# Token scatters of a cross-attention stage, issued one at a time behind exponentials and values products

## The chip, the cores and the metric

The kernel runs on one core of a Trainium2 chip. Its engines are TensorE (PE in the profile, PEld for its weight loads), VectorE (DVE), ScalarE (ACT), GpSimd (POOL) and SyncE (SP, whose queue issues the plain DMAs). The metric is the device time of one launch in microseconds (us); lower is better.

## The reference, cut to what matters

Input x is 32 batches of 256 tokens with 256 features. Three sublayers follow each other, each with a residual sum and a layer norm: self attention with 16 heads and rotary embedding; a differential cross attention (two softmaxes per head over 120 context keys, subtracted with a factor lambda); and a mixture of experts that routes each token to the best 6 of 64 experts.

```
x = layernorm(x + attention(x))
x = layernorm(x + differential_cross_attention(x, ctx))   # 16 heads, 2 softmaxes each, 120 keys
scores = sigmoid(x @ router.T); top_idx = top_k(scores + bias, 6)
x = layernorm(x + sum_of_6_experts(x, top_idx) + shared_mlp(x))
```

To gather the tokens of an expert later, the kernel fills a table in HBM during the cross stage: entry (expert, position) holds a token's number. Each batch has 256 tokens x 6 choices; on chip that is 2 groups of 128 tokens, so 2 x 6 = 12 scatters per batch, each of which writes 128 four-byte entries, one per partition.

## The kernel before, in words

The program has a self stage, a cross stage and an expert stage. In the first two, every engine runs its own instruction list, and semaphores order them. The cross stage works on one batch of 256 tokens per step, and a step holds work of several batches at different depth (a software pipeline): `A` is the batch whose queries and keys are projected and split into three bf16 parts, `B` and `M` those whose row maxima are found, `S` the one with scores, exponentials and values products, `O` the one with output projection and residual, `R` the one with norm, transposition and router, and `Q` the one whose slots are sorted and scattered. The lags against the step number are A 1, B 2, M 3, S 4, O 5, R 6, Q 7, for 32 batches. So Q and S are both on in steps 7 to 35, which are 29 steps. The last three steps with scatters have no S.

A step has eight rounds g = 0 to 7, on TensorE in this order: scores of round g (two heads, both softmaxes; L810, `c_sc`), a set of maximum scores (L828, `c_mx`), and the values product of the round before (L846, `c_pv`), with the projections, transpositions and router products of the other batches in between. ACT turns the scores of a round into exponentials (L1172, `c_exp`), copies two rounds of values to `att_o_raw` (L1182, `c_pvc`), and takes the rest in a written order: in round 3 the first bf16 part (`copy_parts0`, L1205, `c_hi`), in round 5 `oT` (L1306), the second part (`copy_parts1`, L1209, `c_mid`), and the copy of the transposed negative maxima (`att_cross_nmaxT`, L1318, behind TensorE's L1020 by `c_mTp`), and after that the exponentials of round 6. DVE reduces each set of maximum scores (L1434, `c_red`, which TensorE needs before the next set) and normalises the transposed rounds (L1445, L1447, L1456, behind L861 by `c_ot`).

GpSimd has in each step: two small operations on token numbers, the twelve scatters of Q (L1704, from `scatter`), the first subtraction of A (L1751, waits for `c_hi`; its result is wanted by L1209), the second subtraction (L1759, waits for `c_mid`; its end `c_lo` lets SP store the parts), the norm's small operations for O (L1769 to L1776, behind DVE's statistics) and two sums for R (L1783). Its list is run strictly in the order in which it is written. A scatter is an indirect DMA for which GpSimd itself writes the descriptors. `scatter_in_round(Q, S, g, at)` first waits until the exponentials of round g of the batch S are done, and then issues all scatters of `at`.

Of the kernel before, what the change touches and what calls it, by code (L numbers as in the profile page):

```python
# [101 lines left out]
def attention(nc, n_batches, x_in, xT_in, W, ctxT_in, CW, consts, y_out, res_out, z_out, yT_out, table, moe):  # L102
# [24 lines left out]
    for is_q in (True, False):  # L127
        part_of = [pair[0 if is_q else 1] for pair in PAIRS]
        at = 0
# [20 lines left out]
    NGR = 8  # L150
# [9 lines left out]
    C_N_INIT = 9  # L160

    C_STACK_LOADS = []
    for is_q in (True, False):
        part_of = [pair[0 if is_q else 1] for pair in PAIRS]
        at = 0
# [15 lines left out]
    with ExitStack() as ctx:  # L181
# [1453 lines left out]
        def _(pool):  # L1635
# [73 lines left out]

            def scatter_in_round(Q, S, g, at):  # L1710
                if S.on:
                    n_exp = held(pool, NGR * S.n + g + 1)
                    pool.wait_ge(c_init, C_N_INIT)
                    pool.wait_ge(c_exp, n_exp)
                scatter(Q, at)

            def cross_step(at_lag):
# [9 lines left out]
                if Q.on:  # L1727
                    pool.tensor_scalar(tok_f[:, :], tok_f[:, :], float(T), None, ALU.add).then_inc(c_tk, 1)
                    n_tk, n_scat = held(pool, Q.n + 2), held(pool, 16 * TC * TOP * Q.turn)
                    n_now = held(pool, Q.n + 1)  # L1730
                    pool.wait_ge(c_init, C_N_INIT)
                    pool.wait_ge(c_tk, n_tk)
                    if past(Q.n, 3):
                        pool.wait_ge(c_scat[Q.slot], n_scat)
                    pool.tensor_copy(tok_i[:, Q.slot, :], tok_f[:, :]).then_inc(c_tok, 1)
                    if S.on:
                        n_exp = held(pool, NGR * S.n + 1)
                    pool.wait_ge(c_init, C_N_INIT)
                    pool.wait_ge(c_tok, n_now)
                    pool.wait_ge(c_slot, n_now)  # L1740
                    if S.on:
                        pool.wait_ge(c_exp, n_exp)
                    scatter(Q, range(0, 1))
                    scatter_in_round(Q, S, 1, range(1, 3))
                yield
# [6 lines left out]
                if Q.on:  # L1752
                    scatter_in_round(Q, S, 2, range(3, 4))
                    scatter_in_round(Q, S, 3, range(4, 6))
                    scatter_in_round(Q, S, 4, range(6, 7))
                yield
# [3 lines left out]
                if Q.on:  # L1760
                    scatter_in_round(Q, S, 5, range(7, 9))
                    scatter_in_round(Q, S, 6, range(9, 10))
                if O.on:
# [20 lines left out]
                if Q.on:  # L1784
                    scatter_in_round(Q, S, 7, range(10, 12))

# [426 lines left out]
```

## Time and profile before

| | us |
|---|---|
| median of 3 runs (lowest, highest) | 2097.91 (2096.47, 2111.97) |
| the profiled execution | 2095.74 |
| its span, first to last instruction | 2093.9 |
| its time outside of the span | 1.84 |

The page splits the span into 40 slices of 52.3 us. The self stage fills about the first 14 of them, the cross stage those from there to about slice 32, and the expert stage the rest. A row of the timeline gives the start, the duration, the engine, the line and what is written and read; in brackets stands how long the engine was idle before it and what released it. "remote" is a releaser that the profile could not name, "issue" is time in which it shows no wait. Matmul ends are modelled by the profiler.

### The profile page before, as it was taken

To read this page: it belongs to the slowest core of one execution; us is meant where nothing else is said; L and a number is where in the kernel's file an instruction comes from. 1 tells how busy PE (TensorE), PEld (TensorE's weight loads), DVE (VectorE), ACT (ScalarE), POOL (GpSimd) and SP (SyncE) were. 2 spreads that over 40 slices of the span, in tenths; PEclk is the share of its full clock that TensorE was granted. 3 is DMA by queue.
4 is the path that set the end of the run, shared out by engine and by line. 5 is a ranking of instruction groups with operands and counts; after the bars stand their busy time and mean duration, and the time that the engine had idled before them with its cause. 6 is when DMAs were issued, how large, how long until landed. Compare 5 with 4: busy or idle time off the path is not lost. (4 is left out here: it accounts for less than half of the span.)

```text
span 2093.9 us, 45046 instructions
## 1 busy us (share of the span) xinstructions
PE 1740.5 (83%) x14560; PEld 1217.1 (58%) x14560; DVE 1273.1 (61%) x2887; ACT 1083.7 (52%) x1701; POOL 1274.3 (61%) x1303
## 2 busy tenths in 40 slices
PE   4799999999999877888888888887888833999985
PEld 2566666666766644555555555555554422888874
DVE  3566676767677755776767766677766530322265
ACT  1466666666666555665555565565655410111134
POOL 4566776767677421466566565666665564677676
PEclk7899999999999998998888888899887656999998
DMA  5677868778787655555555445555445104787687
GB/s 121 152 178 185 186 175 187 180 190 188 178 194 177 164 119 125 121 107 108 117 111 103 91 100 115 110 106 115 102 91 99 37 25 123 178 201 195 146 286 266
DMA packets 322362, 300.94 MB, mean 144 GB/s; under 512 B 80626, under 2 KB 299572, under 8 KB 313040
## 3 DMA queue, kind: packets, MB, share of 16 engines
q1 hardware_dynamic: 299728, 286.56, 57.4%
q0 software_dynamic: 22528, 13.03, 4.0%
q8 instruction: 59, 0.97, 0.2%
q14 instruction: 47, 0.39, 0.1%
HBM read 187.28 MB, written 111.17 MB: 143 GB/s over the span
## 5 line engine op out<-in xcount | busy, mean ns | idle before, releaser
L1704 POOL DMA_INDIRECT slot_table<-att_cross_tok_i,att_cross_slot_i x384 | 382.2, 995 | 145.0 <-issue 95.8
L1344 DVE TENSOR_REDUCE att_nmax<-self_p_mx 128x2 f32<-128x512 f32 x512 | 329.3, 687 | 205.6 <-PE self_p_mx L628 205.1
L1434 DVE TENSOR_REDUCE att_cross_nmax<-self_p_mx 128x8 f32<-128x960 f32 x256 | 295.5, 1154 | 178.3 <-PE self_p_mx L828 109.8
L1079 ACT ACTIVATE att_probs<-self_p_sc 128x1024 f32<-128x1024 f32 x256 | 261.0, 1020 | 98.8 <-PE self_p_sc L616 96.3
L1172 ACT ACTIVATE att_probs<-self_p_sc 120x1024 f32<-120x1024 f32 x256 | 261.8, 1023 | 43.0 <-PE self_p_sc L810 31.1
L628 PE MATMUL self_p_mx<-att_k_stack,att_q_stack 96*128 96x256 bf16 x1024 | 161.0, 277 | 55.3 <-DMA att_k_stack<-self_k_parts 50.3
L846 PE MATMUL self_p_pv<-att_probs,att_v_aug 120*32 120x256 f32 x2048 | 187.3, 442 | 5.3 <-ACT att_o_raw L1182 4.9
L828 PE MATMUL self_p_mx<-att_k_stack,att_q_stack 48*128 48x120 bf16 x2048 | 112.5, 231 | 83.5 <-DVE att_cross_nmax L1434 52.8
L616 PE MATMUL self_p_sc<-att_q_stack,att_k_stack 99*128 99x256 bf16 x1024 | 158.3, 278 | 11.6 <-ACT att_probs L1079 10.0
L1980 PE MATMUL ffn_ph<-ffn_xT,ffn_sw 128*128 128x256 f32 x512 | 119.2, 387 | 47.9 <-DMA ffn_x_sb<-x_and_gates 47.9
L828 PEld LDWEIGHTS self_p_mx<-att_k_stack,att_q_stack 48*128 48x128 bf16 x2048 | 77.7, 104 | 127.6 <-DVE att_cross_nmax L1434 77.4
L628 PEld LDWEIGHTS self_p_mx<-att_k_stack,att_q_stack 96*128 96x128 bf16 x1024 | 96.1, 98 | 83.8 <-DMA att_k_stack<-self_k_parts 34.8
L1751 POOL TENSOR_TENSOR att_qk_rest<-att_qk,att_parts 128x752 f32<-128x752 f32 x32 | 51.9, 1622 | 151.3 <-ACT att_parts L1205 150.1
L643 PE MATMUL self_p_pv<-att_probs,att_v_aug 128*32 128x256 f32 x2048 | 141.9, 396 | 0.6 <-ACT att_probs L1079 0.6
L616 PEld LDWEIGHTS self_p_sc<-att_q_stack,att_k_stack 99*128 99x128 bf16 x1024 | 87.0, 98 | 91.2 <-ACT att_probs L1079 42.6
L1663 POOL TENSOR_TENSOR att_rope_products<-att_qkb,att_cos_t 128x512 f32<-128x512 f32 x32 | 40.9, 1277 | 154.5 <-ACT att_qkb L1095 154.5
L1971 PE MATMUL ffn_p<-ffn_sw,ffn_hT 128*128 128x256 f32 x512 | 119.3, 387 | 18.6 <-ACT ffn_hT L2010 17.9
L1980 PEld LDWEIGHTS ffn_ph<-ffn_xT,ffn_sw 128*128 128x128 f32 x512 | 97.9, 194 | 61.2 <-issue 48.1
L1182 ACT ACTIVATE att_o_raw<-self_p_pv 128x512 f32<-128x512 f32 x128 | 76.8, 600 | 107.4 <-PE self_p_pv L846 89.0
L810 PE MATMUL self_p_sc<-att_q_stack,att_k_stack 51*128 51x256 bf16 x1024 | 111.6, 301 | 16.6 <-ACT att_probs L1172 16.0
L2095 POOL DMA_INDIRECT expert_sums<-ffn_ye,ffn_slots x64 | 92.2, 1440 | 44.5 <-DMA expert_sums<-ffn_ye,ffn_slots 18.1
L1971 PEld LDWEIGHTS ffn_p<-ffn_sw,ffn_hT 128*128 128x128 f32 x512 | 95.8, 192 | 36.2 <-ACT ffn_hT L2010 23.1
(174 smaller groups left out, 3632.3 us busy)
## 6 DMA issues: line engine op xcount, KB each, us to landing
att_q_stack<-self_q_parts SPq DMA_DIRECT2D x64, 256.0 KB, 5.6
expert_sums<-att_zeros SPq DMA_DIRECT2D x64, 256.0 KB
att_q_stack<-cross_q_parts SPq DMA_DIRECT2D x128, 128.0 KB
ffn_w<-in_ffn_w SPq DMA_DIRECT2D x64, 256.0 KB
ffn_m_sb<-expert_sums SPq DMA_DIRECT2D x32, 512.0 KB, 5.4
self_q_parts<-att_parts SPq DMA_DIRECT2D x32, 384.0 KB, 2.8
self_k_parts<-att_parts SPq DMA_DIRECT2D x32, 384.0 KB, 3.8
att_k_stack<-self_k_parts SPq DMA_DIRECT2D x32, 384.0 KB, 8.0
```

The source lines that it names most:

```text
L616: mm = pe.matmul(p_sc[:, w, kc * T:(kc + 1) * T], k_stack[0:RM, S.slot, k_at:k_at + P], q_stack[0:RM, S.slot, u * T:(u + 1) * T], start=Tr ...
L628: mm = pe.matmul(p_mx[:, m % 2, c * T:(c + 1) * T], q_stack[0:RK, M.slot, q_at:q_at + P], k_stack[0:RK, M.slot, m * T:(m + 1) * T], start= ...
L643: mm = pe.matmul(p_pv[j * SLOT:(j + 1) * SLOT, (p % 2) * T:(p % 2 + 1) * T], v_aug[:, S.slot, kc, u, :], probs[:, (u // 2) % 4, (2 * (u % ...
L828: mm = pe.matmul(p_mx[:, e, (2 * hh + c) * KEYS:(2 * hh + c + 1) * KEYS], q_stack[r:r + C_RK, M.slot, q_at:q_at + P], k_stack[r:r + C_RK, ...
L846: mm = pe.matmul(p_pv[j * SLOT:(j + 1) * SLOT, (g % 2) * T:(g % 2 + 1) * T], v_aug[0:KEYS, S.slot, e, 2 * g + hh, :], probs[0:KEYS, g % 4, ...
L1079: act.activation(probs[:, g % 4, :], p_sc[:, :, :].rearrange("p b n -> p (b n)"), ACT.Exp, scale=SCALE).then_inc(s_exp, 1)
L1172: act.activation(probs[0:KEYS, g % 4, :], p_sc[0:KEYS, :, :].rearrange("p b n -> p (b n)"), ACT.Exp, scale=C_SCALE).then_inc(c_exp, 1)
L1344: dve.tensor_reduce(nmax[:, M.slot, :, m], p_mx[:, m % 2, :].rearrange("p (c k) -> p c k", c=TC), AX_X, ALU.max, negate=True).then_inc(s_r ...
L1434: dve.tensor_reduce(cnmax[:, M.slot, :, :, 2 * m:2 * m + 2].rearrange("p c e h -> p e h c"), p_mx[:, :, 0:4 * KEYS].rearrange("p e (x k) - ...
L1704: pool.indirect_dma_start(out=table[:, :], out_offset=bass.IndirectOffsetOnAxis(ap=slot_i[:, Q.slot, tc, k:k + 1], axis=0), in_=tok_i[:, Q ...
L1971: mm = pe.matmul(p_y[:, tc * DM:(tc + 1) * DM], hT[:, b % 2, k, tc * P:(tc + 1) * P], sw2[:, k, :], start=(k == 0), stop=(k == SK - 1))
L1980: mm = pe.matmul(p_h[:, k // 2, (k % 2) * T:(k % 2 + 1) * T], sw1[:, f, k * P:(k + 1) * P], xT[:, t % 3, f, :], start=(f == 0), stop=(f == ...
```

## The change

The helper that issued a group of scatters behind the exponentials of a round is replaced by two: one waits for the exponentials of round g, the other for the values product of round g (`c_pv`), and each issues one scatter. By position in GpSimd's list:

| place in GpSimd's list | before | after |
|---|---|---|
| ahead of the first subtraction (L1751) | 0 (exp 0); 1, 2 (exp 1) | 0 (exp 0); 1 (exp 1); 2 (values 1); 3 (exp 2); 4 (values 2); 5 (exp 3) |
| ahead of the second subtraction (L1759) | 3 (exp 2); 4, 5 (exp 3); 6 (exp 4) | 6 (exp 4); 7 (values 4) |
| ahead of the norm's operations | 7, 8 (exp 5); 9 (exp 6) | 8 (exp 6); 9 (values 6) |
| at the end | 10, 11 (exp 7) | 10 (exp 7); 11 (values 7) |

```
-            def scatter_in_round(Q, S, g, at):
+            def scatter_behind_exp(Q, S, g, at):
                 if S.on:
                     n_exp = held(pool, NGR * S.n + g + 1)
                     pool.wait_ge(c_init, C_N_INIT)
                     pool.wait_ge(c_exp, n_exp)
-                scatter(Q, at)
+                scatter(Q, range(at, at + 1))
+
+            def scatter_behind_values(Q, S, g, at):
+                if S.on:
+                    n_pv = held(pool, NGR * S.n + g + 1)
+                    pool.wait_ge(c_init, C_N_INIT)
+                    pool.wait_ge(c_pv, n_pv)
+                scatter(Q, range(at, at + 1))
...
-                    scatter_in_round(Q, S, 1, range(1, 3))
+                    scatter_behind_exp(Q, S, 1, 1)
+                    scatter_behind_values(Q, S, 1, 2)
+                    scatter_behind_exp(Q, S, 2, 3)
+                    scatter_behind_values(Q, S, 2, 4)
+                    scatter_behind_exp(Q, S, 3, 5)
...
-                    scatter_in_round(Q, S, 2, range(3, 4))
-                    scatter_in_round(Q, S, 3, range(4, 6))
-                    scatter_in_round(Q, S, 4, range(6, 7))
+                    scatter_behind_exp(Q, S, 4, 6)
+                    scatter_behind_values(Q, S, 4, 7)
...
-                    scatter_in_round(Q, S, 5, range(7, 9))
-                    scatter_in_round(Q, S, 6, range(9, 10))
+                    scatter_behind_exp(Q, S, 6, 8)
+                    scatter_behind_values(Q, S, 6, 9)
...
-                    scatter_in_round(Q, S, 7, range(10, 12))
+                    scatter_behind_exp(Q, S, 7, 10)
+                    scatter_behind_values(Q, S, 7, 11)
```

## Rows read from the trace of the kernel before

**Rows 1.** The page: busy shares, and the scatters' group

```profile
PE 1740.5 (83%) x14560; PEld 1217.1 (58%) x14560; DVE 1273.1 (61%) x2887; ACT 1083.7 (52%) x1701; POOL 1274.3 (61%) x1303
...
L1704 POOL DMA_INDIRECT slot_table<-att_cross_tok_i,att_cross_slot_i x384 | 382.2, 995 | 145.0 <-issue 95.8
```

**Rows 2.** Busy times of two steps, each from one second subtraction to the next

```profile
1224.30:1253.40 29.10, 24.36 (x240) 15.39 (x237) 19.87 (x49) 16.81 (x28) 17.67 (x23) 0.88 0.49 104
1395.70:1422.80 27.10, 22.27 (x233) 14.04 (x233) 19.76 (x50) 16.64 (x28) 17.56 (x23) 0.94 0.60 112
```

**Rows 3.** Waits from 1000 to 1400 us: total, times, longest

```profile
ACT att_o_raw L1182 <- PE self_p_pv L846: 42.5, 18, 3.3
...
ACT att_cross_nmaxT L1318 <- remote: 31.1, 13, 3.0
...
DVE att_cross_o_inv L1445 <- remote: 28.2, 27, 2.4
```

**Rows 4.** Timeline of a cross step before the first scatter

```profile
831.04 0.42 PE L1020 MATMUL self_p_k<-att_identb,att_cross_nmax_parts 128*96 128x128 bf16 x2
...
831.50 0.38 ACT L1318 ACTIVATE att_cross_nmaxT<-self_p_k 96x256 bf16<-96x256 bf16 x1 [7.14 <-PE self_p_k L1020]
```

**Rows 5.** Timeline of GpSimd in the step that starts at about 1230 us

```profile
1239.74 1.04 POOL L1704 DMA_INDIRECT slot_table<-att_cross_tok_i,att_cross_slot_i  x1 [0.87 <-POOL att_cross_tok_i L1735]
...
1242.37 0.98 POOL L1704 DMA_INDIRECT slot_table<-att_cross_tok_i,att_cross_slot_i  x1 [0.30 <-issue]
1246.74 1.62 POOL L1751 TENSOR_TENSOR att_qk_rest<-att_qk,att_parts 128x752 f32<-128x752 f32 x1 [3.39 <-ACT att_parts L1205]
1248.51 1.03 POOL L1704 DMA_INDIRECT slot_table<-att_cross_tok_i,att_cross_slot_i  x1 [0.15 <-issue]
...
1252.40 0.98 POOL L1704 DMA_INDIRECT slot_table<-att_cross_tok_i,att_cross_slot_i  x1 [0.30 <-issue]
1253.39 1.64 POOL L1759 TENSOR_TENSOR att_parts<-att_qk_rest,att_parts 128x752 bf16<-128x752 f32 x1
...
1257.79 0.98 POOL L1704 DMA_INDIRECT slot_table<-att_cross_tok_i,att_cross_slot_i  x1 [0.30 <-issue]
1262.18 0.21 POOL L1769 TENSOR_SCALAR att_cross_var_eps<-att_cross_mv 128x2 f32<-128x2 f32 x1 [3.41 <-issue]
```

**Rows 6.** Timeline of the other engines in the same step

```profile
1242.62 0.60 ACT L1182 ACTIVATE att_o_raw<-self_p_pv 128x512 f32<-128x512 f32 x1 [1.18 <-remote]
...
1247.75 0.66 DVE L1582 CAST att_cross_nmax_parts<-att_cross_nmax 128x64 bf16<-128x64 f32 x1
...
1249.61 0.65 PE L861 MATMUL self_p_tok<-att_ident,att_o_raw 128*128 128x128 f32 x4
...
1250.10 0.28 PE L1020 MATMUL self_p_k<-att_identb,att_cross_nmax_parts 128*96 128x128 bf16 x2
...
1250.57 0.84 ACT L1209 ACTIVATE att_parts<-att_qk_rest 128x752 bf16<-128x752 f32 x1
1250.71 1.16 DVE L1434 TENSOR_REDUCE att_cross_nmax<-self_p_mx 128x8 f32<-128x960 f32 x1
...
1252.82 1.99 PE L1035 MATMUL self_p_q<-att_cross_w_o,att_oT 128*128 128x256 f32 x8
...
1254.30 0.26 DVE L1445 RECIPROCAL att_cross_o_inv<-self_p_tok 128x16 f32<-128x16 f32 x1 [2.42 <-remote]
1254.42 0.38 ACT L1318 ACTIVATE att_cross_nmaxT<-self_p_k 96x256 bf16<-96x256 bf16 x1 [3.01 <-remote]
...
1254.70 1.01 ACT L1172 ACTIVATE att_probs<-self_p_sc 120x1024 f32<-120x1024 f32 x1
...
1255.77 0.39 PE L810 MATMUL self_p_sc<-att_q_stack,att_k_stack 51*128 51x256 bf16 x4 [0.96 <-ACT att_probs L1172]
...
1258.17 0.64 PE L846 MATMUL self_p_pv<-att_probs,att_v_aug 120*32 120x256 f32 x8
...
1260.24 0.60 ACT L1182 ACTIVATE att_o_raw<-self_p_pv 128x512 f32<-128x512 f32 x1 [3.02 <-PE self_p_pv L846]
```

## The prediction, made before the changed kernel ran

> **What bounds the kernel now.** I read the page first. No engine is full: TensorE 83%, GpSimd 61%, VectorE 61%, ScalarE 52% [rows 1]; the edit touches only the cross stage, so I went on to that. The table of busy times by stretch gives the period of one step: 29.10 us, or in some stretches 27.10 us, with TensorE busy for 24.4 and 22.3 us of it and GpSimd for 17.6 [rows 2]. The stage is therefore bound by a chain of handoffs between engines, and the question is which of them are late. The waits by pair over 400 us answer it: ACT stands idle 42.5 us for values products, 31.1 us for the transposed maxima, and DVE 28.2 us for transposed rounds, all three released by TensorE [rows 3]. Per step (about 14 in that stretch) that is 3.0, 2.2 and 2.0 us, though they overlap one another.
>
> The reader should now compare two handoffs of the same kind. Before the first scatter of the program, the transposition L1020 ends at 831.04 + 0.42 = 831.46 and ACT copies at 831.50: 0.04 us [rows 4]. In a step with scatters the same transposition ends at 1250.10 + 0.28 = 1250.38, ACT is free at 1250.57 + 0.84 = 1251.41, and yet it starts at 1254.42: 4.04 us after the producer, 3.01 of them idle. DVE's L1445 is the same: its input ends at 1250.26 and it starts at 1254.30 [rows 6]. Between the two lies a run of four scatters back to back, from 1248.51 to 1253.38; both consumers start 0.9 to 1.0 us after it is over [rows 5, 6]. The same is seen twice more in that step. The copy L1182 starts at 1242.62, while the third scatter of a run is being issued (from 1242.37), and at the step's end the values product ends at 1258.81, a scatter at 1258.77, and ACT starts at 1260.24, 1.43 us late [rows 5, 6]. So the trace reads as if TensorE's completion signals do not get through while a scatter's transfers follow its issue, for about 1 us each; in a run the shadows join up, and the several signals that TensorE gives in rounds 5 and 6 queue behind them. Signals from ACT or DVE to TensorE are prompt: scores L810 start at 1255.77, 0.06 us behind the exponentials of 1254.70, in the shadow or the issue of a scatter [rows 6]. This is an inference from times; the cause is not in the rows.
>
> The Trainium skill, page "SBUF — State Buffer", section "Who interferes with whom", says the opposite: a DMA never contends with a compute engine, and only a VectorE operation that takes the shared port starves descriptor writing. By that rule scatters could stand anywhere and the change would be worth nothing (2098 us). The rule covers data ports, not the passing of signals; the 0.04 against 4.04 us speaks for an effect, so I keep it as a rival.
>
> **The change, part by part.** Nothing is added or removed but semaphore waits: the twelve scatters stay, 384 in all at 995 ns [rows 1]. The waits on exponentials before were mostly void, because GpSimd came to them late. It was held in its list by `c_hi`: scatter 3 was allowed behind the exponentials of round 2, but stood behind the first subtraction, which began at 1246.74 after 3.39 us of idleness. Thus 3 to 6 ran as one block of four [rows 5]. After the change:
>
> *Ahead of the first subtraction.* Scatters 0 and 1 as before. Scatter 2 waits for the values product of round 1, whose signal reached ACT at 1242.62; so it starts at about 1242.7 instead of 1242.37. Scatter 3 follows, to about 1245.0 (two issues of 0.98 with 0.30 between). Scatter 4 waits for values 2, TensorE's own signal, in the shadow of 3: about 1 us after that, 1245.6 to 1246.0. Scatter 5 follows, to about 1248. The first subtraction then starts at 1248.0 instead of 1246.74, 1.3 us late, and takes 1.62 to 1249.6. The user of its result, L1209, starts at 1250.57 because ACT is busy before it, so 0.9 us of cover are left and it costs nothing [rows 5, 6]. DVE's cast at 1247.75 took 0.66 us, ending just after the subtraction; a later subtraction can hold up the four small operations there, and with them the reduction at 1250.71, by up to 1 us; and ACT's copies in rounds 2 and 3 get three more shadows in their neighbourhood. Bounds for both: 0 (TensorE has several us of dense work in these rounds and its consumers have slack) and 1.0 us. I take 0.3, nearer to zero, since a single shadow is shorter than a round of about 2.5 us.
>
> *Between the subtractions.* Two scatters (6, 7) instead of four, with 7 behind TensorE's signal of values 4, so a run cannot build up. The transposed maxima would then pass at once or after one shadow: ACT's idle time of 3.01 us (2.4 on average, 31.1 / 13) falls to at most 1.0 [rows 3, 6]. Not all of that arrives: the next scores L810 stand in TensorE's list behind the projection L1035, which ends at 1252.82 + 1.99 = 1254.81, and they start at 1255.77. So 0.96 us is what this gives before TensorE itself is late next [rows 6]. The reduction L1434 at 1250.71 and the matmuls behind it come no earlier, and if they came earlier too, the bound of this term would be the whole 1.4 to 2.0 us.
>
> *Behind the second subtraction.* It may start at about 1251.5 instead of 1253.39, since GpSimd has nothing else left; SP takes its result in order behind the maxima's rows, so this alone gains nothing. Scatter 8 moves from exponentials 5 to 6 and 9 from exponentials 6 to values 6, ending about 1 us earlier or later than before: GpSimd waited 3.41 us for the norm's statistics at 1262.18, which covers it [rows 5]. The 1.43 us at the step's end stay, because scatter 9 still ends about when values 7 do. Zero. Scatters 10 and 11 stay late behind the norm; zero.
>
> *TensorE's clock.* The step of 29.10 us has a mean granted clock of 0.88 and the one of 27.10 has 0.94 [rows 2]; of the two levels, 1.2 and 2.4 GHz, each step spends part of its time in the lower one. Fewer gaps on TensorE should make more steps like the faster one: between 0 and 2.0 us per step. I take 0.6, nearer to zero, because no row says which gap lowers the clock, and the one at the step's end (1260.24) stays.
>
> Sum per step: 0.96 - 0.3 + 0.6 = 1.3 us, rounded down to 1.2 for the waits that a scatter now has on signals that themselves come late. It counts in the 29 steps with both S and Q: 35 us. Against the profiled execution that is 2095.7 - 35 = 2061; the median of the runs is 2.2 above that execution, so 2063.
>
> **The rivals.** *It gives nothing* (the first rival, also what the named rule says). The shadow sits on whatever signal comes next; twelve scatters cost about the same wherever they lie, so what rounds 5 and 6 win, rounds 2 and 3, now with scatters 3, 4 and 5, lose. For it: ACT waited in rounds 1 to 2 as well (1.18 us at 1242.62). Against it: in the middle of the step the engines have work queued and GpSimd stood idle there. 2098, plus or minus 10.
>
> *It becomes slower: the first subtraction is late.* All of 2 to 5 now stand ahead of it, and two of them wait for TensorE's signals, which are the ones that shadows hold up. Its end was 1246.74 + 1.62 = 1248.36 and ACT's turn for L1209 is at 1250.57, a slack of 2.21 us. If scatters 4 and 5 are each one shadow later than I think, the subtraction ends at about 1251.6 and ACT, which runs its list in order, stands at L1209 with the maxima's copy and the exponentials of round 6 behind it. That is 1.0 us per step over the slack, 29 us: 2127. It decides from a subtraction that ends later than 1250.6. For it: it takes only 0.9 us more than my estimate. Against it: the gain of the second part stays and would pay for most of it, so about 2110 is as likely within this case.
>
> *It becomes much faster:* the gain of the second part arrives in full and most steps reach the 27.10 us of the faster ones: (0.96 + 2.0) x 29 = 86 us, 2012.
>
> **How the numbers follow.** My forecast with its own range 2020 to 2085 has 0.48, the much faster case 0.10, nothing 0.25, slower 0.17. What a measurement of this kernel can tell from no change is about 1%, 21 us: faster means under 2077. Most of the first two cases lie there (0.55), slower than 2119 has 0.14, and 0.31 is left. The range takes in the bounds of the unshown costs, 2018 to 2112; what it leaves out is the end of either extreme case.
>
> **What would show it.** In the profile after: GpSimd's scatters in runs of one or two (three at most); the wait of L1318 with the releaser not named down from 2.4 us per step to under 1.0; the first subtraction starting one to two us later against its `c_hi`, with no wait of L1209 for it; the period near 27.5 to 28; the copies L1182 and L1266 in rounds 2 and 3 with waits up to 1 us. The prediction is wrong if L1318 still waits 2 us in spite of short runs (then the shadow is no such thing), if ACT waits for L1751 (second rival), or if new waits of ACT in rounds 2 to 4 add up to what rounds 5 and 6 win (first rival).

## The result, and the profile after

| | before | after |
|---|---|---|
| median of 18 runs each (us) | 2098.84 | 2117.67 |
| span of the profiled execution | 2093.9 | 2116.3 |
| mean granted clock | 0.901 | 0.901 |

The ratio is 1.0091, with a 95% interval of 1.0073 to 1.0109: slower by 19 us, where 35 us less were forecast. The page after, the busy line and the scatters' group, to be read beside [rows 1]:

```profile
PE 1750.2 (83%) x14560; PEld 1219.9 (58%) x14560; DVE 1305.2 (62%) x2887; ACT 1083.6 (51%) x1701; POOL 1274.3 (60%) x1303
...
L1704 POOL DMA_INDIRECT slot_table<-att_cross_tok_i,att_cross_slot_i x384 | 381.8, 994 | 301.4 <-PE self_p_pv L846 157.5
```

The same instructions ran, 2887 on VectorE, and yet VectorE was busy for 32 us more. That is the line to follow. The waits from 1000 to 1400 us, against [rows 3]:

```profile
POOL slot_table L1704 <- PE self_p_pv L846: 79.7, 30, 5.7
ACT att_probs L1172 <- PE self_p_sc L810: 43.1, 26, 3.6
ACT att_o_raw L1182 <- PE self_p_pv L846: 39.3, 28, 2.5
...
DVE att_cross_nmax L1434 <- remote: 26.5, 12, 2.8
ACT att_cross_gate_e L1278 <- remote: 21.6, 8, 5.3
```

L1318's wait with the releaser not named is gone, as forecast, but L1434 and L1278 have such waits instead. Over 866 to 1600 us these unnamed waits of ACT and DVE sum to 126.4 us before and 125.9 after: they moved and did not shrink.

To see where in a step time was lost, take the starts of the eight exponentials (L1172) in the timeline and average their distances over the 25 steps whose batch `S` is 5 to 29, for the period and for four stretches of a step (us). Below stands how much of each stretch TensorE spent at the lower of its two clock levels, worked out from the mean granted clock (1 less it, times 2, times the length):

| | period | rounds 0 to 3 | 3 to 5 | 5 to 7 | 7 to 0 |
|---|---|---|---|---|---|
| before | 28.50 | 12.41 | 4.83 | 7.09 | 4.18 |
| after | 29.35 | 11.04 | 6.42 | 8.86 | 3.03 |
| at the lower clock, before | 7.4 | 6.5 | 0.3 | 0.5 | 0.0 |
| at the lower clock, after | 7.5 | 2.1 | 1.2 | 4.1 | 0.1 |

2.5 us are won and 3.4 lost; 0.85 us x 29 steps is 25 us, about the difference of the spans (22). The mean clock is the same, but the time at the lower level has moved from rounds 0 to 3 into round 6. Now VectorE by form of instruction, 866 to 1266 us (busy, mean ns of one), first before, then after:

```profile
L1456 DVE TENSOR_TENSOR att_rope_products<-att_cross_o_n 128x128 f32<-128x128 f32 x56 | 27.1, 484 | 1.9
...
L1582 DVE CAST att_cross_nmax_parts<-att_cross_nmax 128x64 bf16<-128x64 f32 x14 | 5.6, 402 | 0.5
```

```profile
L1456 DVE TENSOR_TENSOR att_rope_products<-att_cross_o_n 128x128 f32<-128x128 f32 x54 | 24.0, 444 | 1.9
...
L1582 DVE CAST att_cross_nmax_parts<-att_cross_nmax 128x64 bf16<-128x64 f32 x14 | 12.9, 922 | 0.5
...
L1584 DVE TENSOR_TENSOR att_cross_nmax_rest<-att_cross_nmax,att_cross_nmax_parts 128x64 f32<-128x64 f32 x14 | 11.6, 830 | 0.5
...
L1466 DVE TENSOR_TENSOR att_cross_gate_b<-att_cross_gate,att_cross_e_bias 128x128 f32<-128x128 f32 x14 | 5.5, 390 | 0.5
```

A single L1582 usually takes 0.20 us, L1584 0.22, L1456 and L1466 0.29. The timeline of one step after shows what happens to them:

```profile
1188.05 1.04 POOL L1704 DMA_INDIRECT slot_table<-att_cross_tok_i,att_cross_slot_i  x1 [0.86 <-ACT att_probs L1172]
...
1191.61 1.16 DVE L1434 TENSOR_REDUCE att_cross_nmax<-self_p_mx 128x8 f32<-128x960 f32 x1 [1.90 <-remote]
...
1191.99 0.98 POOL L1704 DMA_INDIRECT slot_table<-att_cross_tok_i,att_cross_slot_i  x1 [0.30 <-issue]
...
1194.02 0.28 ACT L1278 ACTIVATE att_cross_gate_e<-self_p_q 128x128 f32<-128x128 f32 x1 [2.35 <-remote]
...
1196.25 2.34 DVE L1584 TENSOR_TENSOR att_cross_nmax_rest<-att_cross_nmax,att_cross_nmax_parts 128x64 f32<-128x64 f32 x1
...
1196.86 1.64 POOL L1762 TENSOR_TENSOR att_qk_rest<-att_qk,att_parts 128x752 f32<-128x752 f32 x1
...
1198.53 0.83 ACT L1209 ACTIVATE att_parts<-att_qk_rest 128x752 bf16<-128x752 f32 x1 [0.53 <-POOL att_qk_rest L1762]
...
1199.57 0.38 ACT L1318 ACTIVATE att_cross_nmaxT<-self_p_k 96x256 bf16<-96x256 bf16 x1 [0.22 <-PE self_p_k L1020]
...
1200.99 1.62 POOL L1769 TENSOR_TENSOR att_parts<-att_qk_rest,att_parts 128x752 bf16<-128x752 f32 x1
...
1201.65 0.58 PE L828 MATMUL self_p_mx<-att_k_stack,att_q_stack 48*128 48x120 bf16 x8 [1.87 <-DVE att_cross_nmax L1434]
...
1203.17 3.78 PE L1035 MATMUL self_p_q<-att_cross_w_o,att_oT 128*128 128x256 f32 x8
...
1207.53 1.02 ACT L1172 ACTIVATE att_probs<-self_p_sc 120x1024 f32<-120x1024 f32 x1 [3.55 <-PE self_p_sc L810]
```

L1584 takes 2.34 us instead of 0.22 and ends 0.09 us after GpSimd's first subtraction (L1762 in the changed file) does. Its successors on the way to the transposed maxima, and the next reduction, are late by as much, and TensorE stands idle for 1.87 us ahead of L828 until that reduction is done. Then it runs slowly: the granted clock over L1035 is 0.50 here, and L1035 takes 3.78 us, where it took 1.99 at a granted clock of 1.00 in [rows 6]. Both go into the wait of 3.55 us ahead of the exponentials of round 7. L1035 ran mostly at the lower level in 18 of the 25 steps after and in 3 before; its mean went from 2.21 to 3.13 us.

Summed over the timelines of the same 25 steps (duration over the usual one, losses of 0.25 us and more, where a GpSimd subtraction lies beside), the *stretch* of VectorE's operations is 0.64 us a step before and 2.05 after. The first subtraction used to start 0.11 us after its input was ready (`c_hi`) and now starts 3.8 us after, because three more scatters stand ahead of it and some of them wait for values products (GpSimd waits 79.7 us for these in 400; in e1 below, without such waits, the subtraction starts 2.3 us after). There it meets L1584 or L1582 in 19 of 25 steps.

The rows from 1188.05 to 1194.02 show the other loss. The run of four scatters, 3 to 6, between the subtractions is gone, but scatters 0 to 3 now go out back to back in 21 of 25 steps, since their signals have already come when GpSimd gets to them. L1434 and L1278 have their unnamed waits during this run and just behind it: such waits of ACT and DVE were mostly in round 5 before (3.7 us a step) and are mostly in round 3 after (4.3), and there rounds 3 to 5 lose 1.6 us.

### The profile page after: what moved, and what is told of

The parts are those of the page before. It is cut to its first block and busy times, and to the rows that moved or that the text cites. A ratio compares the mean times of both kernels' runs of the same rounds, so it can differ in the third digit from the quotient of the medians.

```text
span 2116.3 us, 45246 instructions
## 1 busy us (share of the span) xinstructions
PE 1750.2 (83%) x14560; PEld 1219.9 (58%) x14560; DVE 1305.2 (62%) x2887; ACT 1083.6 (51%) x1701; POOL 1274.3 (60%) x1303
## 5 line engine op out<-in xcount | busy, mean ns | idle before, releaser
L1434 DVE TENSOR_REDUCE att_cross_nmax<-self_p_mx 128x8 f32<-128x960 f32 x256 | 295.2, 1153 | 170.8 <-PE self_p_mx L828 75.5
L1172 ACT ACTIVATE att_probs<-self_p_sc 120x1024 f32<-120x1024 f32 x256 | 262.2, 1024 | 109.5 <-PE self_p_sc L810 102.6
L828 PE MATMUL self_p_mx<-att_k_stack,att_q_stack 48*128 48x120 bf16 x2048 | 108.5, 231 | 85.0 <-DVE att_cross_nmax L1434 48.9
L828 PEld LDWEIGHTS self_p_mx<-att_k_stack,att_q_stack 48*128 48x128 bf16 x2048 | 75.5, 103 | 123.8 <-DVE att_cross_nmax L1434 72.2
L1182 ACT ACTIVATE att_o_raw<-self_p_pv 128x512 f32<-128x512 f32 x128 | 76.8, 600 | 96.9 <-PE self_p_pv L846 84.1
L810 PE MATMUL self_p_sc<-att_q_stack,att_k_stack 51*128 51x256 bf16 x1024 | 109.5, 296 | 13.8 <-ACT att_probs L1172 13.3
L1762 POOL TENSOR_TENSOR att_qk_rest<-att_qk,att_parts 128x752 f32<-128x752 f32 x32 | 52.2, 1631 | 78.5 <-ACT att_parts L1205 78.0
```

The source lines that it names most:

```text
L828: mm = pe.matmul(p_mx[:, e, (2 * hh + c) * KEYS:(2 * hh + c + 1) * KEYS], q_stack[r:r + C_RK, M.slot, q_at:q_at + P], k_stack[r:r + C_RK, ...
L1172: act.activation(probs[0:KEYS, g % 4, :], p_sc[0:KEYS, :, :].rearrange("p b n -> p (b n)"), ACT.Exp, scale=C_SCALE).then_inc(c_exp, 1)
L1434: dve.tensor_reduce(cnmax[:, M.slot, :, :, 2 * m:2 * m + 2].rearrange("p c e h -> p e h c"), p_mx[:, :, 0:4 * KEYS].rearrange("p e (x k) - ...
```

## The experiments

Beside each of them the kernel before ran on the same chip. Theories 1, 2 and 3 of the expectations are explained in those of e1 and e4, theories C (collision) and L (lateness) in that of e13. They were made on five chips; on two of them, those of e5 to e8 and of e9 to e12, the kernel before takes 1954 us instead of 2100. Ratios are to the kernel before on that chip. "Period" and "stretch" are per step, as above.

| run | before, us | this, us | ratio, 95% | period | stretch |
|---|---|---|---|---|---|
| e1_place | 2101.5 | 2141.2 | 1.021 (1.016 to 1.026) | 30.10 | 1.55 |
| e2_waits | 2101.5 | 2098.2 | 0.999 (0.996 to 1.002) | 28.62 | 0.63 |
| e3_memset | 2101.5 | 2052.1 | one run | 27.83 | 1.34 |
| e4_memset_after | 2101.5 | 2034.0 | one run | 27.17 | 2.41 |
| e5_none | 1954.3 | 1961.2 | one run | 25.51 | 1.10 |
| e6_nosub_before | 1954.3 | 1991.3 | 1.019 (1.015 to 1.022) | 25.30 | 1.24 |
| e7_nosub_after | 1954.3 | 2000.3 | 1.025 (1.022 to 1.027) | 25.43 | 1.49 |
| e8_after_345_memset | 1954.3 | 2006.2 | one run | 25.86 | 2.05 |
| e9_before_again | 1953.4 | 1955.2 | 1.000 (0.996 to 1.003) | 24.02 | 0.32 |
| e10_after_again | 1953.4 | 2071.5 | 1.061 (1.057 to 1.065) | 28.44 | 3.40 |
| e11_five | 1953.4 | 2022.1 | 1.037 (1.032 to 1.042) | 26.42 | 2.11 |
| e12_three | 1953.4 | 2003.5 | 1.026 (1.022 to 1.030) | 26.16 | 1.18 |
| e13_nosubs_before | 2099.0 | 2106.5 | 1.003 (1.001 to 1.006) | 29.15 | 0.01 |
| e14_nosubs_after | 2099.0 | 2058.8 | 0.980 (0.976 to 0.984) | 27.35 | 0.01 |
| e15_fit_after | 2099.0 | 2077.6 | 0.988 (0.984 to 0.993) | 28.15 | 1.44 |
| e16_fit_before | 2099.0 | 2109.1 | 1.006 (1.003 to 1.009) | 29.11 | 0.11 |
| e17_both_clear | 2102.9 | 2059.5 | 0.981 (0.977 to 0.986) | 27.18 | 0.00 |
| e18_second_clear | 2102.9 | 2107.8 | 1.003 (1.001 to 1.006) | 28.70 | 1.55 |

### The two halves of the change: e1, e2

e1 has the new places, all behind exponentials; e2 the old places, one at a time, with the second of a pair behind the values product.

```
 e1: -scatter_behind_values(Q, S, 1, 2)   +scatter_behind_exp(Q, S, 1, 2)     (so for 4, 7, 9 and 11)
 e2: -scatter_in_round(Q, S, 1, range(1, 3))
     +scatter_behind_exp(Q, S, 1, 1)
     +scatter_behind_values(Q, S, 1, 2)       (so for 5, 8 and 11)
```

> The new places (scatters 0 to 5 ahead of the first subtraction, 6 and 7 ahead of the second, 8 and 9 ahead of the norm) with every wait on exponentials, none on values products. Theory 1 (late subtraction: the first subtraction runs into DVE's four small operations on the maxima, L1582 344 to 733 ns and L1584 226 to 1009 ns on average, and so holds the reduction and the matmuls behind it): the places alone do it, 1.005 to 1.015 of before, L1582 and L1584 together again 1.2 us or more. Theory 2 (GpSimd's waits on TensorE's values products, 157.5 us in the changed kernel, make it late at every point): 1.000 or below, since these waits are gone.

> The places of before (0 to 2 ahead of the first subtraction, 3 to 6 between, 7 to 9, 10 and 11), one scatter at a time, with 2, 5, 8 and 11 behind the values product of their round instead of its exponentials. Theory 1 (late subtraction): the first subtraction is on time, L1582 and L1584 stay near 0.35 and 0.23 us, and the time is that of before or up to 1% below it. Theory 2 (the waits on values products): 1.005 or above.

The loss comes with the places: e1 is slower by 2.1%, more than either theory had, and e2 is no different from before, so the waits are no cost by themselves. But e1 does not lose where the changed kernel does. Its rounds 3 to 5 take 8.11 us (4.83 before, 6.42 after) and its rounds 5 to 7 only 6.02, its stretch is smaller (1.55), and the unnamed waits of ACT and DVE from 866 to 1600 us are 199 us, against 137 in e2 on the same chip. In e1 it seems to be held signals that cost most.

### Scatters as work without transfers: e3, e4, e5, e8

In e3 (the kernel before) and e4 (the changed one) each scatter is a write of zeros on GpSimd of about the same length (0.95 us), and in e8 (the changed one) scatters 3 to 5 alone are. e5 is the kernel before without scatters. The table of slots stays empty, or partly empty in e8, and the part behind the last exponentials of the cross stage is 9 to 35 us shorter than in the kernel before (415 us). So the times in the table say little here, and the period is what counts.

```
-pool.indirect_dma_start(out=table[:, :], ...).then_inc(c_scat[Q.slot], 16)
+pool.memset(idle_f[:, :], 0.0).then_inc(c_idle, 1)
```

> The kernel before with each of the twelve scatters replaced by a GpSimd memset of 1024 elements on 128 partitions (about 1 us, no DMA); the slot table is not filled, so the expert stage works on none of the tokens and only the cross stage is read. If the transfers of a scatter hold up TensorE's signals: ACT's copy of the maxima L1318 waits no more than 0.3 us per step (2.2 before), DVE's L1445 neither, and the period of a step falls from 28.5 to 26.5 us or less. If GpSimd's business itself is what holds them up: both waits and the period stay.

> The changed kernel with the scatters replaced by the same memsets (slot table not filled, expert stage on none of the tokens; only the cross stage is read). Theory 1 (late subtraction): as late as with scatters, the collision with L1582 and L1584 stays (1.2 us or more together) and the period is at least 0.7 us above that of the memsets in the places of before. Theory 3 (it is the transfers of scatters 3, 4 and 5, now in rounds 2 and 3, that hold up TensorE's signals there, L1278 waiting 21.6 us in 14 steps): the period is within 0.3 us of that of the memsets in the places of before.

> The kernel before without any scatter (slot table not filled, expert stage on no token; only the cross stage is read). It gives the price of the twelve scatters as a whole. If TensorE's signals are held up by the transfers, and memsets of the same length only added a hold of DVE's port (DVE busy 285 to 326 us in 400): all rounds at the floor that the memsets showed, and the interval from the exponentials of round 6 to 7, 8.2 us with memsets and 2.05 before, falls to 4 or less; period 24 to 25 us. If the stage is bound by something else, period 27 or more.

> The changed kernel with scatters 3, 4 and 5 alone replaced by memsets of about the same length (a quarter of the slot table is not filled; only the cross stage is read). Theory 1: the subtraction is as late as in the changed kernel, the interval from the exponentials of round 6 to 7 stays at 5 us or more. Theory 3: L1278 waits under 0.4 us per step (1.5 in the changed kernel), the interval from 3 to 4 falls from 3.46 to below 2.6 and the one from 4 to 5 from 2.96 to about 2.6, and the period by 1 us or more.

In e3 and e4 no unnamed wait of ACT or DVE is left from 866 to 1600 us, and the period falls by 0.7 us from 28.50 and by 2.2 us from 29.35. On that chip it is therefore the scatter as a DMA, its descriptors and its transfers together, that holds TensorE's signals, and not GpSimd's being busy. The forecast of 26.5 us or less for e3 missed, and e4 is 0.7 us below e3, where theory 1 had 0.7 us or more above it and theory 3 a difference of 0.3 at most. Rounds 6 to 7 took 8.2 us in e3 against 2.05 before. L1035 ran at the lower clock there in all 25 steps, and VectorE was late, 866 to 1266 us:

```profile
L1469 DVE TENSOR_TENSOR att_cross_gate_b<-att_cross_gate,att_cross_e_bias 128x128 f32<-128x128 f32 x14 | 23.7, 1695 | 0.5
L1583 DVE CAST att_cross_nmax_parts<-att_cross_nmax 128x64 bf16<-128x64 f32 x15 | 13.5, 902 | 0.5
```

These are L1466 and L1582 of the kernel before, against the second subtraction and against the writes of zeros. This was the first hint at what costs. In e8 rounds 6 to 7 take 5.18 us, as theory 1 had (5 or more). But e5 and e8 ran on a chip where the kernel before takes 1954 us, so their periods say nothing of the chips at 2100. e5's, 25.51 us, is even longer than the 24.02 of e9 below, which has all its scatters, on another chip of that kind: its second subtraction meets L1456 in 23 of 25 steps. No gain from leaving the scatters out is seen there.

### The first subtraction taken away: e6, e7

The first subtraction works on one element of each partition instead of 752, so that the low parts of q and k are not those of the reference.

```
-pool.tensor_tensor(cqk_rest[:, :], cqk[:, :], cparts[:, 0, :], ALU.subtract)
+pool.tensor_tensor(cqk_rest[:, 0:1], cqk[:, 0:1], cparts[:, 0, 0:1], ALU.subtract)
```

> The kernel before with the first subtraction on one element in place of 752 (the second bf16 part of queries and keys is then wrong). GpSimd has 1.6 us less work per step and does not hold DVE's port there. It was on time and its cover was 2.2 us, so 0.99 to 1.00 of before by every theory.

> The changed kernel with the first subtraction on one element. Theory 1 (the late subtraction in DVE's way makes the loss, 1.2 us more in L1582 and L1584 and 0.2 in L1466 per step): the loss against the same kernel with the places of before vanishes, the two are within 0.3%. Theory 3 (scatters 3 to 5 hold up TensorE's signals in rounds 2 and 3): it is still 0.8% or more above the one with the places of before.

With work taken away both are slower than before. Neither theory had this. The stretch fits it: the second subtraction stretches L1456 in 22 and 24 of 25 steps, where e9 below has 5, and e6 has 0.92 us a step more stretch than e9 at a period longer by 1.28. The two kernels differ by 0.4% (e7 is the slower), and on this chip the placement gains nothing once the first subtraction is gone.

### The same two kernels on a chip without held signals: e9 to e12

e9 and e10 are unchanged. e11 has scatter 5, e12 scatters 3 to 5 behind the first subtraction.

```
 e11: -scatter_behind_exp(Q, S, 3, 5)   ahead of the first subtraction, + the same line behind it
 e12: the same for scatters 3 (exp 2), 4 (values 2) and 5 (exp 3)
```

> The kernel before, unchanged, for a profile taken beside those of e10 to e12. The question is what happened in e5 to e8, where the kernel before ran at 1954 us, and not 2100. If the held signals are a thing of the chip: where it runs at about 2100, the step is 28.5 us long and the subtraction L1318 waits about 2 us with a releaser not named; where it runs at about 1954, the step is near 25.4 us, L1318 waits under 0.3 us, and exponentials of TensorE's scores start 0.05 us after them even with scatters beside. The rival: scatters hold signals on every chip alike, and the 1954 us come from a higher clock alone, so that the step shows the same waits of L1318, a few per cent shorter.

> The changed kernel, unchanged, beside e9. Where the kernel before is at 2100: 1.009 of it, as before. Where it is at 1954 there are no held signals to win or lose by: if all of the loss comes from held signals in other places, the ratio is 1.000 plus or minus 0.003; if the late first subtraction is the cause, the ratio stays at 1.005 or more and the exponentials L1209 wait for L1762; the waits and places alone cost about 0.4% in e7 against e6, which would give 1.004.

> The changed kernel with scatter 5 behind the first subtraction instead of ahead of it, so that five stand ahead as before, one at a time. If the late first subtraction is the cause, its start comes about 1.0 us earlier, the time from the exponentials of round 3 to those of round 5 falls from 6.4 us towards 5.4, and the kernel is at 0.985 to 0.992 of e10 where the kernel before is at 2100 (28.4 us per step). If scatters cost the same wherever they lie (signals held in rounds 2 and 3 instead of 5 and 6), the scatter takes its cost along and the ratio to the kernel before stays at 1.007 to 1.012. Where the kernel before is at 1954, both give the ratio of e10 within 0.003.

> The changed kernel with scatters 3, 4 and 5 behind the first subtraction, three ahead of it. If the late first subtraction is the cause, this one is earlier than in the kernel before, and the kernel is at or below the kernel before (ratio 0.985 to 1.000 where that is at 2100). If scatters cost the same wherever they lie, the ratio stays at 1.005 to 1.015, with what rounds 1 to 3 win lost between rounds 4 and 6. Where the kernel before is at 1954: the ratio of e10 within 0.003, unless the subtraction is what costs there, then 0.995 to 1.000.

In neither e9 nor e10 is there a single wait of ACT or VectorE with the releaser not named between 866 and 1600 us, and L1172 starts 0.04 us behind L810 with scatters on either side: no signals are held there. Still the change costs 6%, 118 us, so on this chip held signals are not what makes it slower. Of the 4.42 us a step, 4.15 lie between rounds 6 and 7 (3.04 to 7.19). One step of e9, then one of e10:

```profile
1210.32 1.66 POOL L1751 TENSOR_TENSOR att_qk_rest<-att_qk,att_parts 128x752 f32<-128x752 f32 x1 [1.67 <-ACT att_parts L1205]
...
1210.84 1.16 DVE L1434 TENSOR_REDUCE att_cross_nmax<-self_p_mx 128x8 f32<-128x960 f32 x1 [0.34 <-PE self_p_mx L828]
...
1212.03 0.20 DVE L1582 CAST att_cross_nmax_parts<-att_cross_nmax 128x64 bf16<-128x64 f32 x1
...
1217.00 1.63 POOL L1759 TENSOR_TENSOR att_parts<-att_qk_rest,att_parts 128x752 bf16<-128x752 f32 x1
...
1217.49 0.35 DVE L1475 MAX8 att_cross_top_v<-att_cross_gate_b 128x8 f32<-128x66 f32 x2
```

```profile
1219.33 1.63 POOL L1762 TENSOR_TENSOR att_qk_rest<-att_qk,att_parts 128x752 f32<-128x752 f32 x1
1219.47 1.64 DVE L1466 TENSOR_TENSOR att_cross_gate_b<-att_cross_gate,att_cross_e_bias 128x128 f32<-128x128 f32 x1
...
1222.24 0.58 PE L828 MATMUL self_p_mx<-att_k_stack,att_q_stack 48*128 48x120 bf16 x8 [1.92 <-DVE att_cross_nmax L1434]
...
1222.84 2.37 DVE L1456 TENSOR_TENSOR att_rope_products<-att_cross_o_n 128x128 f32<-128x128 f32 x1
1223.42 1.63 POOL L1769 TENSOR_TENSOR att_parts<-att_qk_rest,att_parts 128x752 bf16<-128x752 f32 x1
1223.76 3.78 PE L1035 MATMUL self_p_q<-att_cross_w_o,att_oT 128*128 128x256 f32 x8
...
1225.13 1.14 DVE L1434 TENSOR_REDUCE att_cross_nmax<-self_p_mx 128x8 f32<-128x960 f32 x1
...
1228.13 1.02 ACT L1172 ACTIVATE att_probs<-self_p_sc 120x1024 f32<-120x1024 f32 x1 [3.55 <-PE self_p_sc L810]
```

In e9 both subtractions happen to lie beside operations that they don't touch, a reduction from PSUM (L1434, 1.16 us as ever) and a search of maxima (L1475), and the chain of L1582 starts 0.05 us after the first ends. In e10 both hit an operation with two inputs in SBUF, which then ends with the subtraction: 1.35 and 2.08 us lost, the reduction L1434 starts late, and TensorE is idle for 1.92 us ahead of L828. Then it runs L1035 at a granted clock of 0.50, in 3.78 us, so that round 7 is later still. L1035 ran mostly at the lower level in 22 of 25 steps of e10 and in none of e9 (3.44 and 1.99 us on average). What makes the loss of 4.42 us larger than the stretch's growth of 3.08 is thus at least in part the clock. The Trainium skill, page "SBUF — State Buffer", section "Who interferes with whom", names this: VectorE and GpSimd share a port pair, and a VectorE operation with two SBUF inputs contends with a GpSimd instruction that reads SBUF, as does a cast or a `tensor_scalar` in a two-port mode. The trace agrees: L1456, L1466 and L1584 have two such inputs, L1582 is a cast and L1488 a `tensor_scalar` (the profile does not tell their mode), and beside a subtraction the reductions L1434 (1152 to 1156 ns on average in every kernel here) and the maxima L1475 (0.23 us at most) were not stretched.

e11 and e12, at 1.037 and 1.026, contradict what was expected of them (e10 within 0.003, or 0.995 to 1.000 for e12). Fewer scatters ahead helped, by 49 and 68 us, but e12, whose first subtraction stretches nothing, has its second beside the mask L1488 in 24 of 25 steps (+1.23 us each). Its period is 2.14 us longer than e9's and its stretch only 0.86 larger. The loss lies in rounds 0 to 3 (12.70 us against 10.38), with 5.6 us at the lower clock there against 1.6 in e9. What lowers it is not shown.

### Both subtractions away, or only out of the way: e13 to e18

e13 (before) and e14 (after) have both subtractions on one element. The others compute everything, and add waits of GpSimd on what VectorE must have finished:

```
 e15: +pool.wait_ge(c_gc, n_gate)     # 5 * R.n + 3: behind L1466, ahead of the first subtraction
      +pool.wait_ge(c_on, n_o1)       # 4 * S.n + 2: behind L1456, ahead of the second
 e16: the kernel before with the second of these waits
 e17: e15, but ahead of the second: +pool.wait_ge(c_mask, R.n + 1)    behind L1488
 e18: the changed kernel with this wait on c_mask alone
```

> The kernel before with both subtractions of the cross stage (L1751 and L1759) on one element of each partition instead of 752, so that the low parts of q and k stay unset; all waits and scatters are as they were. Theory C (collision): VectorE's operations with SBUF inputs are stretched by a GpSimd subtraction that runs beside them, 0.3 to 0.6 us a step in the kernel before; with neither subtraction that is 0, and the kernel is at 0.975 to 1.000 of the one before, unlike e6, where the second subtraction was left and hit L1456 in nearly every step (1.0185). Theory L (the first subtraction's lateness alone): as here it is not late, 0.99 to 1.00; e6 stays unexplained.

> The changed kernel with both subtractions on one element. Theory C: no VectorE operation is stretched, and what is left is the placement's own worth. Where scatters hold no signals of TensorE (the kernel before at 1954) it equals e13 within 0.5%; where they do (the kernel before at 2100) the forecast gain is there, 0.5 to 1.2 us a step, 0.983 to 0.993 of e13. If held signals cost the same wherever the scatters lie, it equals e13 there too; if new waits of the scatters cost by themselves, it is 0.5% or more above e13 on either.

> The changed kernel with two waits more on GpSimd: the first subtraction also behind VectorE's L1466 of this step, the second behind L1456 of the step's second normalisation, so that those two operations can't meet a subtraction. Both subtractions are full and if anything later. Theory C: stretched time falls from 2.05 us (chip with the kernel before at 2100) or 3.40 us (at 1954) a step to under 1.0, and the kernel gains 1 to 3 us a step on e0, the changed kernel: 0.985 to 1.000 of the kernel before where that is at 2100, 1.00 to 1.02 where it is at 1954. Theory L: later subtractions make it slower than the changed kernel, over 1.009 and 1.061.

> The kernel before with the second subtraction also behind L1456 of the step's second normalisation. Theory C: its 0.44 us a step (at 2100) or 0.32 us (at 1954) of stretched L1456 go, 0.2 to 0.6 us a step less: 0.993 to 0.998 of the kernel before. Theory L: nothing or slightly slower, 1.000 to 1.003.

> The changed kernel with the first subtraction behind VectorE's L1466, as in e15, and the second behind the mask L1488 instead of behind L1456. In e15 the second started at 1217.61 in the step read, beside L1488 (1217.47), and stretched it from 0.23 to 1.85 us in nearly every step (1.44 us a step); here it can meet neither. Theory C: stretched time under 0.4 us a step, and 0.5 to 1.5 us a step less than e15: 0.967 to 0.985 of the kernel before where that is at 2100, 0.985 to 1.005 where it is at 1954. Theory L: the second subtraction comes at the same time as in e15, so the same ratio as e15, 0.988; where the kernel before is at 1954 it would be over 1.02.

> The changed kernel with the second subtraction alone moved behind the mask L1488; the first may meet L1582, L1584 and L1466 as in the changed kernel (1.54 us a step where the kernel before is at 2100). Theory C: the stretched L1456 goes (0.46 us a step), the rest stays: 0.3 to 0.8 us a step less than the changed kernel, 0.998 to 1.006 of the kernel before, and slower than e17 by 1 us a step or more. Theory L: the first subtraction is as early as in the changed kernel and earlier than in e17, so this one is faster than e17.

e14 against e13 is 0.977, 48 us: the forecast gain is there, and more, once no subtraction meets VectorE. On the chip of e6 and e7, where no signals are held, the same placement gained nothing, which speaks for the held signals as what it is good for. e13 missed: 1.003 where 0.975 to 1.000 was expected. Without any stretch, unnamed waits of ACT and DVE are 202 us from 866 to 1600 us there (126 before; L1172 has some of up to 3.8 us), and L1035 ran mostly at the lower clock in 18 of 25 steps. So the collision is not the only thing that can slow round 6, and e13 is a poor kernel to measure the gain from: against the kernel before on its chip, e14 is 40 us faster.

e15 to e18 decide between collision and lateness. In e15 and e17 the first subtraction is later than in the changed kernel, and L1209 really waits for it, and yet they are faster than both kernels. The waits of e17 from 1000 to 1400 us:

```profile
DVE att_cross_nmax L1434 <- remote: 59.4, 29, 3.6
...
ACT att_parts L1209 <- POOL att_qk_rest L1766: 15.1, 12, 2.4
```

In e15 the ratio came as theory C expected, but the stretch of 1.44 us did not (under 1.0): the second subtraction only changed its victim. One step of it, then VectorE's group in e17, 866 to 1266 us:

```profile
1217.47 1.85 DVE L1488 TENSOR_SCALAR att_cross_mask<-att_cross_without 128x128 bf16<-128x128 f32 x1
1217.61 1.62 POOL L1777 TENSOR_TENSOR att_parts<-att_qk_rest,att_parts 128x752 bf16<-128x752 f32 x1
```

```profile
L1456 DVE TENSOR_TENSOR att_rope_products<-att_cross_o_n 128x128 f32<-128x128 f32 x59 | 17.4, 296 | 2.0
...
L1488 DVE TENSOR_SCALAR att_cross_mask<-att_cross_without 128x128 bf16<-128x128 f32 x15 | 3.6, 240 | 1.6
```

e17, with both clear, is at 0.981 (0.977 to 0.986), 43 us below the kernel before and the best version that computes everything. e18 keeps the earlier first subtraction with its 1.55 us of stretch and is 48 us slower than e17; L1035 ran mostly at the lower clock in 10 of its 25 steps and in 2 of e17's. So the collision of the first subtraction costs 1.5 us a step, its lateness nothing that shows. One rival is left here: the wait that moves the subtraction also moves scatters 6 and 7 behind it. Against it stands e14, where nothing collides, those scatters do not wait for L1466, and the time is about the same on another chip (0.980 of the kernel before, against 0.981). For the kernel before a clear second subtraction is no cure (e16, 1.006, where theory C had 0.993 to 0.998 and L up to 1.003): the stretch went to 0.11, but signals are held at L1182 instead (108 us of unnamed waits from 866 to 1600 us, against 9.5 before), it seems because the scatters behind the subtraction moved with it. e17 was not run on a chip of the other kind.

## Why the prediction was wrong, point by point

*The bound and the held signals.* Right in part for the chips on which the kernel before takes 2100 us: L1318's unnamed wait (2.4 us each time) is gone. That runs of scatters would be of three at most is wrong: the run of four only moved, from scatters 3 to 6 to scatters 0 to 3, and the held signals with it. Without collisions the order is worth 1.8 us a step in the periods of e13 and e14 (29.15 and 27.35), but 1.15 against the kernel before (28.50), where 1.2 was forecast. On chips at 1954 us there is no such effect.

*The rival "it gives nothing"*, that the held signals move and don't vanish, is right about their sum (126.4 and 125.9 us). Its conclusion does not follow from that: in e17 the sum is even larger, 172 us, at a shorter period. What counts is who waits. The new waits of L1434 and L1278 make rounds 3 to 5 longer by 1.6 us (6.42 after and 6.40 in e17, against 4.83), and the rest of the step wins 2.9 (e17).

*Ahead of the first subtraction.* This is the step that failed. The prediction read [rows 6] L1582 at 0.66 us, "ending just after the subtraction", and said that a later one "can hold up the four small operations there"; it then put this together with the shadows in rounds 2 and 3 under one bound of 0 to 1.0 us and took 0.3. Measured: the stretch grows by 1.41 us a step (0.64 to 2.05), and the two terms apart are 1.5 us (e18 against e17) and 1.6 us (rounds 3 to 5, at the run of scatters 0 to 3). The subtraction was to start 1.3 us later and starts 3.7 us later against `c_hi` (0.11 to 3.83): GpSimd waits 2.7 us each time for a values product (79.7 / 30), where the forecast had about 1 us. This delay was counted against L1209's cover only, on ACT. And the 0.66 us of L1582 in [rows 6] were a stretch already, for alone it takes 0.20. Of VectorE's list it was asked that something might be late, not which operations the subtraction would now lie beside: it left the reduction L1434, which it can't touch, for L1582, L1584 and L1466, which it can. With the collisions taken away the kernel is at 2059.5 (e17), where 2063 was forecast. That the two agree is in part luck: e17 loses 1.6 us in rounds 3 to 5, where the forecast had 0.3 for that and the collision together, and wins 2.9 elsewhere.

*Behind the second subtraction: zero.* Wrong in what it says of the step's end. The subtraction itself changed little, as it starts 0.9 us after L1209 (1.5 before) and stretches L1456 by 0.46 us a step (0.44 before); clearing it makes the period 28.70 (e18, on another chip of the same kind) instead of 29.35. But the wait at the step's end was to stay, and the time from round 7 to round 0 is 1.15 us shorter (4.18 to 3.03).

*The rival "slower: the first subtraction is late"* forecast 2127 by ACT's wait at L1209. That wait is 5.5 us in 400 us after, 0.4 a step, and up to 15 in e17 without harm. The rival is right that the later subtraction costs, and wrong about how.

*TensorE's clock* (a gain of 0.6 us a step forecast). No gain came: the mean stayed at 0.901, and of a step 7.4 us were at the lower level before and 7.5 after. But 3.9 us of them now lie in round 6 (0.4 before), and L1035 takes 0.92 us a step more there, while rounds 0 to 3 got 1.4 us shorter. The forecast took the step's mean and did not ask which work would run at the lower level. In e17 and e9, with shorter steps, the mean is 0.916 and 0.940.

*The range.* The prediction says that 2020 to 2085 takes in the bounds of the unshown costs, 2018 to 2112. It does not, and how 2112 comes about isn't worked out; the time measured, 2117.67, lies above both.

## What to carry to other kernels

When an instruction on GpSimd moves, list what VectorE runs beside its old and its new place: here operations with two inputs in SBUF, casts and a `tensor_scalar` ended with the subtraction they met, while a reduction from PSUM and a search of maxima did not notice. A mean duration above the usual one (484 against 290 ns for L1456 in the kernel before) is the sign, and it stands in the table by form before anything is changed. A wait that makes GpSimd late on purpose, behind the operation it would hit, can be worth more than the earliest start (48 us between e18 and e17). When TensorE has to stand idle, look at the granted clock of the work behind the gap too, for the mean of the whole run can hide it (0.901 twice here, with L1035 at 2.21 and 3.13 us). And a gain that rests on a mechanism inferred from one chip's trace should be tried on another chip.

## What the runs showed of the hardware that was not expected

Chips differ, and not only in clock. (Each chip was used at one time only, so a difference of the hour is not excluded.) Of the five chips of the experiments, two take 1954 us for the kernel before and the others 2099 to 2103. The self stage is the same (the first exponentials of the cross stage start at 775.6 us in e9, and at 777.5 in e13), but the cross step is 24.02 against 28.5 us, with no held signal between 866 and 1600 us against 126 us of such waits. What holds TensorE's signals behind a scatter on some chips stays open; that it is the scatter as a DMA and not GpSimd's being busy, e3 and e4 show for theirs.

A VectorE operation that starts up to 0.6 us ahead of a subtraction's recorded start is stretched too (L1584 at 1196.25, L1762 at 1196.86), and then loses more, 2.1 us, than the 1.6 us that the subtraction takes. GpSimd's writes of zeros, which read nothing, stretch VectorE's casts as well, from 0.20 to 0.88 and 0.78 us (L1583 and L1588 in e3). Taking away the first subtraction's work made the kernel before 1.9% slower (e6).
